# A token mixer on one core: paired w2 products, another scratch layout, later tables and another table of places

## The chip, the cores and the metric
The kernel runs on one core of a Trainium2 chip. The metric is the device time of one execution in microseconds; the time of a kernel is the median of its runs. The engines are TensorE (PE; its weight loads are PEld), VectorE (DVE), ScalarE (ACT), GpSimd (POOL) and SyncE (SP), which here issues every DMA transfer.

## The reference
The input `x` has 32 images of 96 channels and 56x56 points. Layer 0 is a convolution block. Layer 1 is a token mixer with a Fourier transform over the 3136 tokens of an image, and an MLP. The change lies in layer 1 alone.

```python
x = _L0_conv_ref(x, ...)              # 1x1, depthwise 3x3, 1x1, each with batch norm; plus x
t = _to_tokens(x)                     # (32, 3136, 96)
t = t + _L1_attn_ref(_ln_t(t), ...)
t = t + _L1_ffn_ref(_ln_t(t), ...)    # 96 -> 384 -> 96, factors rounded to an 8-bit float
x = _from_tokens(t, x)

def _L1_attn_ref(x, w1, ..., r, i, rb, ib, w2, ...):
    h = jnp.einsum('bnc,hc->bnh', x, w1)               # 192 columns
    h = jax.nn.relu(_bn(h, ...))
    X = jnp.fft.fft(h, axis=1, norm='ortho')
    rd = jnp.diagonal(r)
    idg = jnp.diagonal(i)
    xr = jax.nn.relu(X.real * rd - X.imag * idg + rb)
    xi = jax.nn.relu(X.imag * rd + X.real * idg + ib)
    y = jnp.fft.ifft(xr + 1j * xi, axis=1, norm='ortho').real.astype(jnp.float32)
    o = jnp.einsum('bnh,ch->bnc', y, w2)
    return _bn(o, ...)
```

## The kernel before
The convolution stages come first and leave `z3_scratch`. Then `tokens_stage` takes the images one by one. The Fourier transform of 3136 = 56 x 56 tokens is done in two stages of small products each way; since `h` is real, 29 frequencies `k1` of the first axis are enough. An image passes these steps:

- `load_in`, `act_bn3`, `pool_y`: seven chunks of 8 rows are loaded, batch-normed and added; `store_t` keeps the sum in HBM for the residual.
- `mean1`, `act_square1`, `square1`, `dve_var1`, `act_std1`, `row1`: the statistics of the first layer norm. `row1` (`load_row`, four small transfers) puts the standard deviations into row 96 of `y`.
- `w1` (14 products of 193 columns in pairs), `dve_rstd1`, `act_h`, `stage1`, `act_a`, `store_a`: in seven pieces, w1 with the layer norm, then the first transform stage into `bank_w_s`; ScalarE copies the piece into one of the two halves of `a`, and SyncE stores it to `a_scratch`. The rows of `a` are (q, k): q is one of four groups of 32 rows, k the frequency. A piece may overwrite its half once the piece two before it has landed in HBM (`a_scalar` waits for `st_a[p - 2]`).
- `load_b`: four transfers load `bt` back as (q, j) rows, a run of 192 elements for each row and frequency. The first waits until all seven pieces have landed.
- `spectrum` (6 groups; those named wide take the channels 128 to 191, two frequencies in one product), `act_scaled`, `dve_real`, `pool_imag`, `act_relu`, `dve_fold`: the second transform stage into `bank_x`, the diagonal weights and the ReLU. `fold_vector` writes `zp` (channels 0 to 127, one slot a frequency) or `zq` (wide: channels 128 to 191 of two neighbouring frequencies in the two halves of the rows).
- `w2` (8 groups of four frequencies, the last of one), `dve_wz`, `stage3`, `dve_c`, `store_c`, `load_d`: the w2 product into `bank_c`, a copy to `wz`, the first stage of the way back, a copy to `cc`, and a second trip through HBM, `c_scratch`.
- `stage4` (7 chunks of four products), `dve_residual`: the last stage into `bank_o`; VectorE adds the residual `tb`. There is one `bank_o`, so each chunk of stage 4 waits for the residual before it.
- `mean2` to `dve_rstd2`, `spread_mean`, `spread_rstd`, `dve_centre`, `dve_norm`: the second layer norm; the spread products bring mean and rstd to all channel rows, and VectorE centres (`xc`) and norms (`yq`).
- `mlp1`, `act_h16`, `dve_bias1`, `dve_relu1`, `mlp2`, `act_o`, `dve_bias2`, `pool_out`, `store_out`: the MLP and the output.

Each engine's order is a table of numbers. `PLACES` gives every part of every step a place; a turn is `NT` = 2000 places, a place of 4321 stands for place 321 of the turn two after the image entered. An engine runs through the places of a turn and does what stands there for each of the five images in flight (`LAGS`), as the `..._turn` functions show. Nothing is timed: an engine takes the next step in this order and waits on its semaphores. So a step that waits holds up all that follows on its engine, on SyncE the transfers too.

Before the first turn, SyncE waits for three constants that VectorE sets (`s_init`, among them the memset of `d`), loads six tables (`t1c` 896 KB, `t4c` 1568 KB, `g2c`, `g3c`, and two parts of `sel_d`), and only then the first image. TensorE and VectorE wait for all tables (`s_const`) before their first turn.

The w2 product of a group before; `w2q` holds the weights of the channels 128 to 191 twice, for the upper half of the rows in its columns 0 to 95 and for the lower half in 96 to 191, with zeros elsewhere:

```python
        for j, k1 in enumerate(ks_of(u)):
            o, e = CB[0:TP, 0, j * C:j * C + C], k1 % 2
            nc.tensor.matmul(o, zp[:, k1 // 8 % 2, k1 % 8, :], w2p[:, :], start=True, stop=False)
            ins = nc.tensor.matmul(o, zq[:, k1 // 2 % 8, :], w2q[:, e * C:e * C + C], start=False, stop=True)
```

## Time and profile before

| | before |
|---|---|
| median of 3 runs | 5265.94 us (5251.65 to 5277.84) |
| the profiled execution | 5252.71 us, span 5250.9 us |
| TensorE clock, mean of the span | 0.958 |
| busy share PE / PEld / DVE / ACT / POOL | 91 / 61 / 68 / 65 / 49% |
| DMA: bytes moved, mean rate | 1072 MB, 204 GB/s |
| tokens stage | 2567 us to the end |

The span runs from the first to the last instruction, the time of an execution lies a little above it. A view of windows gives for each stretch how long each engine was busy; the table of waits gives how long an engine stood idle before a line, and whose result ended the wait; the chain of waits is followed back from the last instruction. In a timeline a row stands for a run of like instructions: its start, the time from its start to its end, and in brackets the idle time of the engine before it. A clock of 1.00 is 2.4 GHz and 0.50 is 1.2 GHz.

### The profile page before, as it was taken

Reading aid. Unit: us, or ns where it says so; the run is one execution under the profiler, and the core shown is the slowest. Engines: PE = TensorE matmul, PEld = TensorE weight load, DVE = VectorE, ACT = ScalarE, POOL = GpSimd, SP = SyncE. Lnnn points to the kernel's source line nnn. Section 1 sums busy time; section 2 is a strip of 40 time slices with the busy share of each in tenths; the row PEclk is TensorE's granted clock in tenths of the full one; section 3 lists DMA queues with packets and bytes.
Section 4 is the critical chain, followed back from the end, with each engine's and each line's share of the span. In section 5 each row is a group of like instructions: output and inputs, shape, how many; then the busy total and the mean of one; then the engine's idle time right before and its main releaser. Section 6 shows DMA issues by size and latency. Waiting matters only on the chain.

```text
span 5250.9 us, 153775 instructions
## 1 busy us (share of the span) xinstructions
PE 4775.0 (91%) x63188; PEld 3204.1 (61%) x63188; DVE 3551.9 (68%) x6475; ACT 3387.4 (65%) x5511; POOL 2574.2 (49%) x1508
## 2 busy tenths in 40 slices
PE   8989999999999989999678888888898898889886
PEld 8955555555555544444356666666666666666663
DVE  1156776776778766777427777777777777777776
ACT  4455655565566568888447667676677676777663
POOL 0067777777777756666323333333333333334331
PEclk9989999999999999999769999999999999999997
DMA  7656776777777689999556676776776766776762
GB/s 159 164 144 178 192 182 181 192 183 182 191 185 186 172 315 415 412 419 418 212 146 176 182 183 176 190 182 180 188 187 178 187 182 179 193 184 181 188 156 64
DMA packets 505463, 1072.16 MB, mean 204 GB/s; under 512 B 182240, under 2 KB 330240, under 8 KB 471872
## 3 DMA queue, kind: packets, MB, share of 16 engines
q1 hardware_dynamic: 504768, 1062.33, 70.7%
q8 instruction: 505, 8.27, 0.7%
q14 instruction: 190, 1.56, 0.1%
HBM read 557.40 MB, written 484.44 MB: 198 GB/s over the span
## 4 chain that ended last, share of the span: by engine, by line
PE 31%; DVE 8%; DMA 6%; issue 4%; ACT 2%; SPq 1%; POOL 0%; DVEq 0%; POOLq 0%; ACTq 0%
PE bank_w_s L1456 6%; DMA bt<-a_scratch 4%; PE bank_o L1434 3%; PE bank_w_s L1465 3%; PE bank_x L1409 3%; PE bank_c L1417 3%; PE bank_c L1418 2%; PE bank_c L1424 2%; PE bank_x L1406 2%; PE bank_l L1333 2%; PE bank_l L1390 1%; PE bank_o L1445 1%; DVE zq L1693 1%; PE bank_l L1349 1%; DVE wz L1794 1%
## 5 line engine op out<-in xcount | busy, mean ns | idle before, releaser
L772 POOL TENSOR_TENSOR hlo<-h,hhi 128x1682 f16<-128x1682 f32 x288 | 977.6, 3394 | 376.8 <-DVE hhi L825 376.8
L785 DVE BATCH_NORM_STATS2 stats<-z 128x6 f32<-128x392 f32 x1152 | 597.1, 560 | 437.9 <-ACT z L725 427.8
L735 ACT ACTIVATE h<-c1ps,s 128x1568 f32<-128x1568 f32 x288 | 479.3, 1664 | 629.3 <-PE c1ps L651 629.3
L683 PE MATMUL dwps<-hhi,taps 64*64 64x392 f16 x13824 | 692.9, 331 | 9.5 <-issue 9.4
L683 PE MATMUL dwps<-hlo,taps 64*64 64x392 f16 x13824 | 684.5, 328 | 4.4 <-issue 4.4
L1649 POOL TENSOR_TENSOR s_plus<-d_minus,imag_scaled 128x448 f32<-128x448 f32 (+1 forms) x192 | 203.6, 1060 | 897.1 <-ACT imag_scaled L1516 897.1
L1658 POOL TENSOR_TENSOR onat<-tb,o 96x448 f32<-96x448 f32 x224 | 262.7, 1173 | 643.3 <-DVE o L1718 643.3
L930 ACT ACTIVATE z2m<-z2m,s 128x784 f32<-128x784 f32 x512 | 489.5, 1029 | 104.0 <-DMA z2m<-z_scratch 103.4
L954 POOL TENSOR_TENSOR h_split<-z2m,h_split 128x1568 f16<-128x1568 f32 x128 | 405.2, 3166 | 264.6 <-DVE h_split L993 264.6
L683 PEld LDWEIGHTS dwps<-hhi,taps 64*64 64x64 f16 x13824 | 381.1, 106 | 251.1 <-issue 104.9
L683 PEld LDWEIGHTS dwps<-hlo,taps 64*64 64x64 f16 x13824 | 406.4, 106 | 185.3 <-issue 7.3
L1592 ACT ACTIVATE h<-bank_w_s,rt 128x192 f32<-128x192 f32 x896 | 319.9, 425 | 141.0 <-DVE rt L1724 138.4
L1642 POOL TENSOR_TENSOR y<-zin,x_tok 96x448 f32<-96x448 f32 x224 | 302.2, 1362 | 200.9 <-ACT zin L1598 196.3
L1456 PE MATMUL bank_w_s<-w1a,y 97*128 97x193 f32 x1792 | 381.4, 358 | 15.9 <-ACT a L1586 8.4
L1531 ACT ACTIVATE h<-bank_l 128x448 f16<-128x448 f32 x672 | 340.2, 542 | 80.8 <-PE bank_l L1390 72.6
L201 POOL TENSOR_TENSOR xlo<-xin,x_packed 96x448 f16<-96x448 f32 x224 | 233.7, 1044 | 287.6 <-ACT x_packed L192 287.5
L966 PE MATMUL pps<-z2m,w3T 128*96 128x392 f32 x1024 | 360.4, 495 | 15.1 <-ACT z2m L930 15.1
L1456 PEld LDWEIGHTS bank_w_s<-w1a,y 97*128 97x128 f32 x1792 | 334.0, 211 | 43.2 <-ACT a L1586 14.1
L1417 PE MATMUL bank_c<-w2p,zp 128*112 128x96 f32 x1856 | 347.8, 270 | 10.0 <-DVE cc L1802 10.0
L1418 PE MATMUL bank_c<-w2q,zq 128*112 128x96 f32 x1856 | 337.1, 264 | 0.0
L1434 PE MATMUL bank_o<-t4c,d 128*96 128x112 f32 x1792 | 246.9, 286 | 98.0 <-DVE tb L1748 93.4
L1586 ACT ACTIVATE a<-bank_w_s 128x768 f32<-128x768 f32 x224 | 181.7, 811 | 223.9 <-PE bank_w_s L1465 219.1
(234 smaller groups left out, 10110.9 us busy)
## 6 DMA issues: line engine op xcount, KB each, us to landing
z_scratch<-z SPq DMA_DIRECT2D x1152, 196.0 KB, 3.3
z2m<-z_scratch SPq DMA_DIRECT2D x64, 1960.0 KB, 15.9
...
a_scratch<-a SPq DMA_DIRECT2D x896, 96.0 KB, 1.9
...
t_scratch<-y SPq DMA_DIRECT2D x32, 1344.0 KB, 6.4
c_scratch<-cc SPq DMA_DIRECT2D x128, 336.0 KB, 3.7
d<-c_scratch SPq DMA_DIRECT2D x128, 336.0 KB, 3.9
```

The costliest lines, as they stand in the source:

```text
L683: ins = nc.tensor.matmul(dw[64 * j:64 * j + 64, r, g, 0:QN], taps[half, u, da, dx, :, :].rearrange("p y c -> p (y c)"), part[half, s, a0:a ...
L735: nc.scalar.activation(to, src, ACT.Relu, bias=s1[:, 1, u:u + 1], scale=s1[:, 0, u:u + 1]).then_inc(h_ready, 1)
L772: nc.gpsimd.tensor_tensor(to, h, hi, ALU.subtract).then_inc(lo_ready, 1)
L785: nc.vector.bn_stats(stats[:, i, v, at:at + 6], z2[:, v % 3, g, r, :]).then_inc(s_stat, 1)
L930: nc.scalar.activation(v, v, ACT.Relu, bias=s2[:, 1, t:t + 1], scale=s2[:, 0, t:t + 1]).then_inc(h2_ready, 1)
L954: nc.gpsimd.tensor_tensor(lo, h32, hi, ALU.subtract).then_inc(lo_ready, 1)
L966: nc.tensor.matmul(banks[m], w3T[:, t, :], z2m[:, c // 2, 4 * m + t, cols], start=(t == 0), stop=False)
L1417: nc.tensor.matmul(o, zp[:, k1 // 8 % 2, k1 % 8, :], w2p[:, :], start=True, stop=False)
L1418: ins = nc.tensor.matmul(o, zq[:, k1 // 2 % 8, :], w2q[:, e * C:e * C + C], start=False, stop=True)
L1434: ins = nc.tensor.matmul(OB[0:C, 0, k * TP:k * TP + TP], d[:, j, :], t4c[:, j, :], start=True, stop=True)
L1456: ins = nc.tensor.matmul(WS[:, g % 2, e * (H + 1):(e + 1) * (H + 1)], both, w1a[:, :], start=True, stop=True)
L1531: nc.scalar.activation(h16[:, c % 2, q, :], LL[k % 2][:, 0, 0:CH], ACT.Copy).then_inc(h16_done, 1)
```

## The change
Four things.

**The w2 product** of a group begins with the `zq` part, two frequencies at once: `zq` of a pair is the stationary operand and 192 columns of `w2q` the moving one, so that both frequencies' columns of `bank_c` are written by one product. Then each frequency's `zp` part is added. A group of four has 2 products of 192 columns and 4 of 96 where it had 8 of 96.

**The first scratch** becomes `(NB, 128, NJ, H)`, by the rows of `a` as they lie. A piece is stored by one transfer of 128 rows instead of four of 32, and `load_b` issues four transfers of 28 rows, one for each q, instead of one of 112.

**The tables** come behind the first image: `t1c` after chunk 3, the others after chunk 6, each with its own semaphore, which is waited for where it is first used. SyncE starts at once, and the memset of `d` is the last of the three.

**The places** are all new (of the table two lines are shown).

```diff
-    a_d = nc.dram_tensor("a_scratch", (NB, KP, 4, NJ, H), F32, kind="Internal").ap()
+    a_d = nc.dram_tensor("a_scratch", (NB, 128, NJ, H), F32, kind="Internal").ap()
...
-PLACES = {'load_in': (790, 792, 1059, 1276, 1342, 1628, 1944),
...
+PLACES = {'load_in': (212, 561, 689, 855, 903, 940, 974),
...
-    s_const, s_init, s_sel, s_settled = sem("tables_loaded"), sem("constants_set"), sem("rows_table"), sem("settled")
+    s_init, s_sel, s_settled = sem("constants_set"), sem("rows_table_loaded"), sem("settled")
+    s_t1, s_g, s_t4 = sem("t1_loaded"), sem("g2_g3_loaded"), sem("t4_loaded")
...
         sp.dma_start(xin[:, c % 3, :], x[n, :, cols]).then_inc(ld_in[c % 3], 16)
+        if isinstance(n, int) and n == 0:
+            load_tables(sp, c)
+
+    def load_tables(sp, c):
+        if c == 3:
+            sp.dma_start(t1c[:, :, :], t1_d.rearrange("p (j c) -> p j c", j=NJ)).then_inc(s_t1, 16)
+        if c == 6:
+            sp.dma_start(g2c[:, :], g2_d).then_inc(s_g, 16)
+            sp.dma_start(g3c[:, :], g3_d).then_inc(s_g, 16)
+            sp.dma_start(t4c[:, :, :], t4_d.rearrange("p (j c) -> p j c", j=NJ)).then_inc(s_t4, 16)
...
         if k == 0:
             for p in range(NP4):
-                sp.wait_ge(st_a[p], f * 64 + 64)
+                sp.wait_ge(st_a[p], f * 16 + 16)
...
-        src = a_d[f, k0:k0 + n].rearrange("k q j c -> (q j) k c")
-        sp.dma_start(bt[:, k0:k0 + n, :], src).then_inc(ld_b[k], 16)
+        for q in range(4):
+            src = a_d[f, 32 * q + k0:32 * q + k0 + n].rearrange("k j c -> j k c")
+            sp.dma_start(bt[NJ * q:NJ * q + NJ, k0:k0 + n, :], src).then_inc(ld_b[k], 16)
...
-        for q in range(4):
-            v = a[32 * q:32 * q + 32, (par + p) % 2, :, :].rearrange("k b x -> k (b x)")
-            to = a_d[f, :, q, 4 * p:4 * p + 4, :].rearrange("k j c -> k (j c)")
-            sp.dma_start(to, v).then_inc(st_a[p], 16)
+        v = a[:, (par + p) % 2, :, :].rearrange("p b x -> p (b x)")
+        sp.dma_start(a_d[f, :, 4 * p:4 * p + 4, :].rearrange("p j c -> p (j c)"), v).then_inc(st_a[p], 16)
...
     def _(sp):
-        sp.wait_ge(s_init, 3)
         sp.dma_start(im_t[:, :, :, :].rearrange("p a s c -> p (a s c)")[:, 0:4 * C], sel_d[:, 0:4 * C]).then_inc(s_sel, 16)
-        sp.dma_start(t1c[:, :, :], t1_d.rearrange("p (j c) -> p j c", j=NJ)).then_inc(s_const, 16)
-        sp.dma_start(t4c[:, :, :], t4_d.rearrange("p (j c) -> p j c", j=NJ)).then_inc(s_const, 16)
-        sp.dma_start(g2c[:, :], g2_d).then_inc(s_const, 16)
-        sp.dma_start(g3c[:, :], g3_d).then_inc(s_const, 16)
-        sp.dma_start(part[:, :], sel_d[:, 4 * C:4 * C + 2]).then_inc(s_const, 16)
+        sp.dma_start(part[:, :], sel_d[:, 4 * C:4 * C + 2]).then_inc(s_sel, 16)
         turns(sp, sync_turn)
...
-        for j, k1 in enumerate(ks_of(u)):
-            o, e = CB[0:TP, 0, j * C:j * C + C], k1 % 2
-            nc.tensor.matmul(o, zp[:, k1 // 8 % 2, k1 % 8, :], w2p[:, :], start=True, stop=False)
-            ins = nc.tensor.matmul(o, zq[:, k1 // 2 % 8, :], w2q[:, e * C:e * C + C], start=False, stop=True)
+        ks = ks_of(u)
+        for j in range(0, len(ks), 2):
+            w = len(ks[j:j + 2]) * C
+            nc.tensor.matmul(CB[0:TP, 0, j * C:j * C + w], zq[:, ks[j] // 2 % 8, :], w2q[:, 0:w], start=(j == 0),
+                             stop=False)
+        for j, k1 in enumerate(ks):
+            ins = nc.tensor.matmul(CB[0:TP, 0, j * C:j * C + C], zp[:, k1 // 8 % 2, k1 % 8, :], w2p[:, :],
+                                   start=False, stop=(j == len(ks) - 1))
...
     def _(dve):
-        nc.vector.memset(d[:, :, :], 0.0).then_inc(s_init, 1)
         nc.vector.memset(y[:, :, :, :, W:64], 1.0).then_inc(s_init, 1)
         nc.vector.memset(va[:, :, :], 1.0).then_inc(s_init, 1)
-        dve.wait_ge(s_sel, 16)
+        nc.vector.memset(d[:, :, :], 0.0).then_inc(s_init, 1)
+        dve.wait_ge(s_sel, 32)
```

What the new places do to the order is seen at three places of a steady turn. The first is VectorE at the start of stage 4: `tb` is the residual, `zq` the wide fold, `va` the variance of the next image, `rt` the reciprocal for its w1. Before:

```order
L1699 TENSOR_SCALAR va<-va 128x4x56
L1718 TENSOR_SCALAR o<-o,fqb 96x448
L1748 SCALAR_TENSOR_TENSOR tb<-bank_o,w2shift,tb 96x8x56
L1693 SCALAR_TENSOR_TENSOR zq<-d_minus,s_plus 128x8x56 x2
L1748 SCALAR_TENSOR_TENSOR tb<-bank_o,w2shift,tb 96x8x56 x2
L1724 RECIPROCAL rt<-bank_w_s 128x2
```

and after:

```order
L1718 TENSOR_SCALAR va<-va 128x4x56
L1737 TENSOR_SCALAR o<-o,fqb 96x448
L1767 SCALAR_TENSOR_TENSOR tb<-bank_o,w2shift,tb 96x8x56 x3
L1712 SCALAR_TENSOR_TENSOR zq<-d_minus,s_plus 128x8x56 x2
L1743 RECIPROCAL rt<-bank_w_s 128x2
```

The wide fold moved from behind the first residual to behind the third. TensorE's order around it is the same in both: three chunks of stage 4, four w1 products, a chunk, w2 group 0.

The second is where the MLP of one image begins beside the w2 groups 2 and 3 of the next. On TensorE, from the spread of the rstd (`rstd_parts`) to the first mlp1 (`yq`), before:

```order
L1362 MATMUL bank_l<-rstd_parts,sel 96x224 x4
L1465 MATMUL bank_w_s<-h,t1c 64x192 x8
L1390 MATMUL bank_l<-yq,fq 128x448 x2
L1456 MATMUL bank_w_s<-w1a,y 128x193 x4
L1390 MATMUL bank_l<-yq,fq 128x448
L1424 MATMUL bank_c<-wz,g3c 112x384
```

and after:

```order
L1371 MATMUL bank_l<-rstd_parts,sel 96x224 x4
L1485 MATMUL bank_w_s<-h,t1c 64x192 x8
L1440 MATMUL bank_c<-wz,g3c 112x384
L1400 MATMUL bank_l<-yq,fq 128x448 x2
L1474 MATMUL bank_w_s<-w1a,y 128x193 x2
```

Stage 3 of group 2 moved ahead of the first mlp1. A little later on VectorE, from the last wide fold (`zq`, 7 slots) to the copy `wz` of w2 group 3 and the second pair of centrings (`xc`), before:

```order
L1693 SCALAR_TENSOR_TENSOR zq<-d_minus,s_plus 128x7x56 x2
L1724 RECIPROCAL rt<-bank_w_s 128x2
L1794 COPY wz<-bank_c 112x384
L1724 RECIPROCAL rt<-bank_w_s 128x2
L1729 TENSOR_TENSOR xc<-tb,bank_l 96x448 x2
```

and after:

```order
L1813 COPY wz<-bank_c 112x384
L1724 TENSOR_SCALAR h<-h,fqb 128x448
L1743 RECIPROCAL rt<-bank_w_s 128x2
L1748 TENSOR_TENSOR xc<-tb,bank_l 96x448 x2
L1743 RECIPROCAL rt<-bank_w_s 128x2
L1821 COPY cc<-bank_c 112x384
L1757 TENSOR_TENSOR yq<-xc,bank_l 96x448 x2
L1731 TENSOR_SCALAR hq<-h 128x1344
L1712 SCALAR_TENSOR_TENSOR zq<-d_minus,s_plus 128x7x56 x2
```

The fold moved behind the copy, the centrings and the norms.

The third is SyncE, from the sixth store of `a` to the first two loads of `bt`, before:

```order
L1275 DMA a_scratch<-a 32x768 x4
L1268 DMA tb<-t_scratch 96x512
L1254 DMA c_scratch<-cc 112x8x96
L1268 DMA tb<-t_scratch 96x512
L1275 DMA a_scratch<-a 32x768 x4
L1261 DMA d<-c_scratch 32x2688
L1249 DMA bt<-a_scratch 112x8x192
L1254 DMA c_scratch<-cc 112x8x96
L1249 DMA bt<-a_scratch 112x8x192
```

and after:

```order
L1268 DMA c_scratch<-cc 112x8x96
L1287 DMA a_scratch<-a 128x768
L1275 DMA d<-c_scratch 32x2688
L1287 DMA a_scratch<-a 128x768
L1282 DMA tb<-t_scratch 96x512
L1263 DMA bt<-a_scratch 28x8x192 x4
L1282 DMA tb<-t_scratch 96x512 x2
L1263 DMA bt<-a_scratch 28x8x192 x4
```

The load of `d` moved ahead of the last store of `a`, and the store of `cc` between the two loads of `bt` is gone from there. Also on SyncE, the store of the image (`t_scratch<-y`, 1344 KB) moved from between the fifth and the sixth store of `a` to between the second and the third:

```order
L1287 DMA a_scratch<-a 128x768
L1268 DMA c_scratch<-cc 112x8x96
L1293 DMA t_scratch<-y 96x3584
L1287 DMA a_scratch<-a 128x768
```

These last rows are of after; in a turn all seven chunks of the next image are loaded ahead of them, where before the last chunk was loaded three stores later.

## Rows read from the trace of the kernel before

**Rows 1.** The page, busy time and share of the span of TensorE, with its instructions.
```profile
PE 4775.0 (91%) x63188; PEld 3204.1 (61%) x63188; DVE 3551.9 (68%) x6475; ACT 3387.4 (65%) x5511; POOL 2574.2 (49%) x1508
```
**Rows 2.** Row transfers on SyncE (first and last start), and ten steady turns by engine.
```profile
L1239 SPq DMA_DIRECT2D y<-va x128: 511/657/731, 2603.3 to 5044.7; - x128
...
3947.00:4737.00 790.00, 708.13 (x6597) 531.72 (x6596) 588.63 (x1225) 556.59 (x1036) 300.50 (x260) 0.97 0.70 184
```
**Rows 3.** Waits of TensorE in these ten turns: us in total, times, longest.
```profile
PE bank_o L1434 <- DVE tb L1748: 28.5, 20, 2.1
...
PE bank_x L1409 <- DMA bt<-a_scratch: 5.5, 8, 1.2
```
**Rows 4.** The chain of waits, w2 and w1 products: start, us, instructions merged.
```profile
4228.73 0.20 PE bank_c L1417 x2
...
4263.05 2.27 PE bank_w_s L1456 x8
...
4271.06 1.32 PE bank_w_s L1456 x8
```
**Rows 5.** Timeline of VectorE, residuals and folds of a steady turn.
```profile
4258.47 2.20 DVE L1693 SCALAR_TENSOR_TENSOR zq<-d_minus,s_plus 128x448 f32<-128x448 f32 x2
4260.59 0.67 DVE L1748 SCALAR_TENSOR_TENSOR tb<-bank_o,w2shift,tb 96x448 f32<-96x448 f32 x1
...
4298.61 1.76 DVE L1693 SCALAR_TENSOR_TENSOR zq<-d_minus,s_plus 128x392 f32<-128x392 f32 x2 [1.22 <-PE bank_c L1418]
```
**Rows 6.** Timeline of TensorE in the same turn, with its waits in brackets.
```profile
4258.53 1.01 PE L1434 MATMUL bank_o<-t4c,d 128*96 128x112 f32 x8 [0.84 <-DVE tb L1748]
4261.32 1.73 PE L1434 MATMUL bank_o<-t4c,d 128*96 128x112 f32 x8 [1.78 <-DVE tb L1748]
...
4291.74 0.54 PE L1390 MATMUL bank_l<-yq,fq 96*128 96x448 fp8e5 x2 [0.72 <-DVE yq L1738]
...
4300.96 0.90 PE L1424 MATMUL bank_c<-wz,g3c 112*112 112x384 f32 x2 [0.67 <-DVE wz L1794]
4302.17 0.44 PE L1362 MATMUL bank_l<-rstd_parts,sel 12*96 12x224 bf16 x4 [0.32 <-DVE xc L1729]
```
**Rows 7.** Timeline of the start and of a steady turn, issues on SyncE.
```profile
2603.26 2.75 SPq L1239 DMA_DIRECT2D y<-va  x4
2607.11 2.94 PE L1456 MATMUL bank_w_s<-w1a,y 97*128 97x193 f32 x8 [5.89 <-DMA y<-va]
...
4257.03 2.59 SPq L1239 DMA_DIRECT2D y<-va  x4
...
4311.94 2.12 SPq L1275 DMA_DIRECT2D a_scratch<-a  x4
```
**Rows 8.** The chain's transfers; the page's: count, KB each, median us to landing.
```profile
4233.86 1.89 DMA a_scratch<-a
...
4235.99 6.00 DMA bt<-a_scratch
...
a_scratch<-a SPq DMA_DIRECT2D x896, 96.0 KB, 1.9
...
t_scratch<-y SPq DMA_DIRECT2D x32, 1344.0 KB, 6.4
...
x_tok<-in_x_dram SPq DMA_DIRECT2D x224, 168.0 KB, 3.9
```
**Rows 9.** Timeline of the start of the tokens stage.
```profile
2566.81 2.30 DVE L1840 MEMSET d<- 128x2688 f32 x1 [1.13 <-PEq L870]
...
2570.35 0.33 SPq L1310 DMA_DIRECT2D imag_scaled<-table_sel  x1
...
2581.49 0.76 ACT L1598 ACTIVATE zin<-zin,s 96x448 f32<-96x448 f32 x1 [16.82 <-DMA x_tok<-in_x_dram]
```
**Rows 10.** Timeline of ScalarE, copies of pieces 3 and 5 into `a`.
```profile
4284.89 0.81 ACT L1586 ACTIVATE a<-bank_w_s 128x768 f32<-128x768 f32 x1 [1.78 <-PE bank_w_s L1465]
...
4296.79 0.81 ACT L1586 ACTIVATE a<-bank_w_s 128x768 f32<-128x768 f32 x1
```

135 lines of the change are left out of this document (72 added, 63 removed).

## The prediction
> **What bounds the kernel now.** I read the page first: TensorE is busy 91% of the span [rows 1]. The change lies in the tokens stage, which begins at 2567 us with the first memset [rows 9] and runs 32 images through a pipeline, one per turn. The LN1 row transfer of the first image is issued at 2603.3 and the last at 5044.7 [rows 2]; less the 2 us between the first and the fourth transfer of a row, that is 2439 us in 31 turns, 78.7 us a turn. In ten steady turns (790 us) TensorE is busy 708 us, VectorE 589, ScalarE 557, and the DMA engines 70% [rows 2]. So TensorE is the bound and waits 8.2 us a turn. The table of TensorE's waits says on whom [rows 3]: 28.5 us in ten turns on the residual of VectorE (stage 4 and the residual hand one bank back and forth) and 5.5 on the loads of `bt`; smaller ones stand singly in [rows 6]. An edit pays if it shortens TensorE's work or one of these waits, and only so far as nothing else is late by then.
>
> **The w2 product.** Before, each of the 29 frequencies takes two products of 96 columns, each with its own weights; the trace has two instructions for one fp32 product. In the chain such a pair takes 0.20 us, 98 ns an instruction, while eight instructions of 193 columns take 1.32 us, 165 ns each [rows 4]. 165 ns for 193 columns would be 82 ns for 96, so at 96 columns something other than the columns sets the pace; the weights in between are what is left. A group of four frequencies has 16 instructions: 16 x 98 = 1.57 us. After, it has 4 of 192 columns and 8 of 96: 4 x 165 + 8 x 98 = 1.44 us. That is 0.13 us less in each of seven full groups, **0.9 us a turn**. Bounds: 0, if a column costs 98/96 ns in these products whatever the weights; 1.8 us, if the eight narrow ones ran at 82 ns (1.57 - 0.66 - 0.66 = 0.25 us a group). I stay at 0.9, because the narrow ones keep their own weights.
> The Trainium skill (TensorE: Matmul & The Clock Gate, The mechanism) says that weight loads overlap running matmuls only where the row groups differ, and (LDWEIGHTS) gives P/1.2 ns for P columns, an estimate of 93 ns for our 112. Strictly in series with an 82 ns product that would be 175 ns an instruction; the trace has 98 [rows 4], so here they overlap and the measurement decides. In series, the 14 saved loads (28 instructions) would be worth 2.6 us a turn instead of 0.9.
>
> **Stage 4 and the wide fold.** At this place VectorE does one residual, then the two `zq` halves of the fold (2.20 us), then the next residual [rows 5]; TensorE's third stage 4 waits 1.78 us for that residual [rows 6]. After, the fold stands behind three residuals. The second stage 4 starts at 4258.53, takes 0.95, the residual 0.6 and the handover 0.1: the third starts at 4260.2 instead of 4261.32, **1.1 us earlier**. The next work, w1 of the new image, needs the row transfer: in turn 0 TensorE starts 1.1 us after the last of the four issues has ended (2606.01, 2607.11), and here that gives 4257.03 + 2.59 + 1.1 = 4260.7 [rows 7], before TensorE comes (4261.1). What is late next is the folded `zq`: the third residual ends at about 4261.8, the fold at 4264.0, and w2 comes behind four w1 products (1.3) and a stage 4 (0.8), at 4263.3: a new wait of 0.7, which I reduce to 0.5, because part of the w1 work there runs at the lower clock. VectorE's reciprocals for w1 stand behind the fold too and delay ScalarE's `h`, whose user, stage 1, comes only after w2 and another stage 4. Price: 1.1 - 0.5 = **-0.6**, bounds -1.8 and 0.
>
> **The waits before mlp1 and behind w2 group 3.** TensorE waits 0.72 us for `yq` before the first mlp1 [rows 6]. After, stage 3 of group 2 stands in this gap (an 0.8 us piece whose `wz` was copied before the norms), **-0.7**. Further on VectorE waits 1.22 us with the last wide fold for w2 group 3 and folds for 1.76 us, and only then copies `wz` [rows 5]; stage 3 waits 0.67 and the spread of the rstd 0.32 [rows 6]. After, the copy and the two centrings come first and the fold later; w2 group 4, its user, is still over 4 us away. **-1.0**. Bounds of both together: 0 and -1.7.
> Sum so far: 0.9 + 0.6 + 0.7 + 1.0 = 3.2 us a turn.
>
> **The first scratch.** Four stores of 96 KB become one of 384 KB, and each load of 672 KB becomes four of 168 KB. The last piece's path is the one that matters: TensorE's last stage 1, the copy, store, wait, load, spectrum. Four issues take 2.12 us of SyncE [rows 7], and the last store lands 1.89 us after its issue [rows 8]; one issue takes 0.3, and between 1.9 us for 96 KB and 6.4 for 1344 KB [rows 8] the line gives 2.9 for 384 KB. So 4.0 becomes 3.2 us: -0.8. The load: 6.00 us where it is clear [rows 8]; four issues put its last quarter 1.0 to 1.3 us behind the first, but the bytes and runs are the same and the first starts as before; I take +0.5, bounds 0 and +1.3. The load of `d` that stood between the last store and the load (the order above) is issued before it now, which takes 336 KB out of the way: up to -0.5. Together about -0.8, but the path also has less work to hide behind: two w2 groups (0.3) lie on it. SyncE's order elsewhere: in the new one the 1344 KB store of the image stands ahead of the third store of `a`, the fourth load of `bt` behind the sixth image chunk; both have slack (below). I book 0 for the whole path and +0.3 for the shortened cover, bounds -0.55 (today's wait for `bt` at the first spectrum group is gone [rows 3]) and +1.5.
> The Trainium skill (DMA: Bandwidth & Descriptors, Why a DMA increments its semaphore by 16 and not by 1) says a transfer uses the largest number of engines up to 16 that divides its outermost size: 16 for the old 112, 14 for the new 28. No row here shows such a size. By this rule the 6.00 us become 6.9.
>
> **The start.** SyncE no longer waits for the memsets, and the tables do not stand ahead of the image: the first transfer goes at 2566.8 instead of 2570.35, four issues less are ahead, and the first chunk, used at 2581.49 [rows 9], comes some 10 us sooner. But the 896 KB table lies between chunks 3 and 4, and the 1568 KB table plus the image's store ahead of the row transfer. I take **-6 us once**, bounds -10 and 0.
>
> **The sum.** 3.2 a turn, less 0.3 for the `bt` cover, less 0.4 because three of the w2 groups lie in a stretch where VectorE is the late one (the chain between two loads of `bt` runs over it), makes 2.5; 31 turns give 78 us, and with the start 84. The profiled execution took 5252.7 us (span 5250.9), so 5169. It stands 13 us under the median of the three runs (5265.9), at their low end; of this I add half, 6: **5175 us**.
>
> **Rivals.**
> *The clock gives back more.* In the steady turns the granted clock is 0.97 on average [rows 2]: 6% of the time at 1.2 GHz, 4.7 us a turn, 2.4 of them lost. One such stretch begins at 4261, right behind the two waits of stage 4: eight w1 instructions take 2.27 instead of 1.32 us [rows 4]. The change removes waits right ahead of it and of the next (4302, behind the waits of 0.67 and 0.32). If both stretches go, 31 x 2.4 = 74 us: 5101; half of it, 5138. For it: the places agree. Against: some waits remain at both (0.8 and 0.7 us in stage 4). Chance 0.12.
> *Gains absorbed.* Store of `a` number 3 now stands behind the 1344 KB store. ScalarE's copy of piece 5 into the same half waits for its landing; today the copies of pieces 3 and 5 start at 4284.89 and 4296.79, 11.9 us apart [rows 10]; 0.8 for the copy, 6.4 and 2.9 for the transfers make 10.1. For it: DMA is busy 70%. Chance 0.18.
> *The new places do nothing, the w2 product gains 0.* The waits wander to the next late engine, as VectorE is busy 75%: start and little else, 5240 to 5275. Against: the four places are read one by one. Chance 0.13.
> *Slower: the quarter loads run one behind the other.* If each of the four costs what a 168 KB transfer costs alone, 3.9 us [rows 8], a load of `bt` takes 15.6 instead of 6.0: +9.6 on a path that TensorE already waits for, less 2.5: +7.1 a turn, 5175 + 31 x 9.6 = 5473. It decides from a load longer by 3.5 us on, where the 84 us are eaten and 26 more lost. Against: four stores are issued within 2.12 us and the last lands 1.89 us after its own issue [rows 7, 8], so transfers of one queue overlap. Chance 0.07.
> *The forecast*, 5135 to 5215: 0.50.
>
> **How the numbers follow.** The range 5095 to 5240 holds the forecast, the clock and the absorbed case: 8 in 10. A measurement of this kernel can tell 0.5% from no change, 26 us: below 5239.6 is faster, 0.80; up to 5292 the same, 0.13; above, slower, 0.07.
>
> **What would show it.** Rows of a steady turn: w2 groups of 12 instructions in 1.44 us and 165 ns for the wide ones; stage 4's wait on the residual at 1.8 us a turn instead of 2.85, and at most 0.7 of a new wait of w2 for `zq`; no wait of stage 3 behind w2 group 3 nor of the first mlp1; waits for `bt` below 1.5 us a turn; a turn of 76.2 us; the first w1 at about 2601 instead of 2607. I am wrong if the waits are gone and the turn is still over 77 (then look at ScalarE's copy of piece 5 and at the loads of `bt`), or if the wide products take over 190 ns.

## The result and the profile after

| | before | after |
|---|---|---|
| median | 5264.56 us (5251.65 to 5277.84, 4 runs) | 5099.26 us (5094.76 to 5113.47, 4 runs) |
| span of the profiled execution | 5250.9 us | 5092.8 us |
| TensorE clock, mean of the span | 0.958 | 0.972 |

The ratio is 0.9697, with an interval of 0.9679 to 0.9714: 3.0% faster. The forecast was 5175 us with a range of 5095 to 5240. The direction was right and the time lies inside the range, at its edge; but the gain is 165 us where its sum had 84 (5175 stands 90 under the median before).

The page after, TensorE and the other engines [as rows 1], and the row transfers on SyncE [as rows 2]:
```profile
PE 4692.9 (92%) x62292; PEld 3120.1 (61%) x62292; DVE 3398.0 (67%) x6475; ACT 3389.3 (67%) x5511; POOL 2513.4 (49%) x1508
...
L1252 SPq DMA_DIRECT2D y<-va x128: 510/658/732, 2596.5 to 4887.3; - x128
```
A turn takes (4887.3 - 2596.5 - 2) / 31 = 73.8 us instead of 78.7: 4.9 less, where 2.5 was forecast. The first row transfer goes at 2596.5 instead of 2603.3: 6.8 once, where 6 was forecast. 31 x 4.86 + 6.8 is 157.5 of the 158.1 us between the spans, so nearly all of it is in the turn.

To see where a turn changed I took 25 turns, the fifth to the twenty-ninth, of every kernel, with the mean length of a turn as the measure. The view of windows gives them in one row each: stretch, its length, busy time of TensorE, its weight loads, VectorE, ScalarE, GpSimd, then clock, DMA share, GB/s. Before, then after:
```profile
2918.10:4885.30 1967.20, 1764.62 (x16370) 1323.36 (x16369) 1461.44 (x3043) 1378.57 (x2568) 746.79 (x647) 0.96 0.70 184
```
```profile
2891.80:4737.60 1845.80, 1702.67 (x15679) 1257.56 (x15678) 1339.45 (x3047) 1383.64 (x2575) 699.58 (x649) 0.99 0.74 196
```
Divided by 25: TensorE was busy 70.6 us and idle 8.1; now it is busy 68.1 and idle 5.7. So the gain has two halves, 2.5 less work and 2.4 less waiting. The table of TensorE's waits in ten turns (us in total, times, longest), 3830 to 4568 in after [as rows 3]:
```profile
PE bank_o L1452 <- DVE tb L1767: 17.6, 20, 1.7
PE bank_x L1421 <- DMA bt<-a_scratch: 8.8, 10, 1.7
PE bank_l L1342 <- ACT sq L1573: 8.1, 10, 0.8
PE bank_c L1440 <- DVE wz L1813: 7.9, 19, 0.7
PE bank_l L1400 <- ACT h L1550: 4.8, 9, 0.5
PE bank_l L1371 <- DVE xc L1748: 4.8, 10, 0.5
```
And four lines of the same table of before, 3947 to 4737, that [rows 3] does not show:
```profile
PE bank_c L1424 <- DVE wz L1794: 14.2, 25, 0.9
PE bank_l L1390 <- DVE yq L1738: 6.7, 10, 0.7
PE bank_l L1362 <- DVE xc L1729: 3.1, 10, 0.3
PE bank_x L1406 <- DMA bt<-a_scratch: 2.8, 5, 1.0
```
The residual `tb` cost 28.5 and costs 17.6, as foreseen (2.85 to 1.8 a turn). The waits for `yq` are gone. Those for the copy `wz` fell from 14.2 to 7.9. `bt`, two lines in before, costs as much as it did: 8.3 and 8.8.

The clock has a part of its own. The trace's record of the granted clock, added up over the same 25 turns as their own row transfers cut them (in before from 2908.4 to 4883.3 us), has 146.8 us at 1.2 GHz before, in 32 stretches, and 30.7 us in 7 after: 5.9 and 1.2 us a turn. A stretch at half clock costs at most half its length, so at most 2.9 and 0.6 us a turn are lost.

### The profile page after: what moved, and what is told of

Its sections match the earlier page's. It is cut to its first block, busy times and chain, and to the rows that moved or that the text cites. A ratio compares the mean times of both kernels' runs of the same rounds, so it can differ in the third digit from the quotient of the medians.

```text
span 5092.8 us, 151731 instructions
## 1 busy us (share of the span) xinstructions
PE 4692.9 (92%) x62292; PEld 3120.1 (61%) x62292; DVE 3398.0 (67%) x6475; ACT 3389.3 (67%) x5511; POOL 2513.4 (49%) x1508
## 3 DMA queue, kind: packets, MB, share of 16 engines
q1 hardware_dynamic: 499136, 1062.31, 72.5%
## 4 chain that ended last, share of the span: by engine, by line
PE 32%; DMA 8%; DVE 5%; issue 2%; ACT 1%; SPq 1%; POOL 1%; DVEq 0%; POOLq 0%; ACTq 0%
PE bank_w_s L1474 6%; PE bank_o L1452 4%; PE bank_x L1421 4%; DMA bt<-a_scratch 3%; PE bank_w_s L1485 3%; PE bank_c L1440 2%; PE bank_c L1433 2%; PE bank_c L1430 2%; DMA a_scratch<-a 2%; PE bank_l L1400 2%; PE bank_l L1342 2%; DMA tb<-t_scratch 1%; PE bank_x L1418 1%; PE bank_l L1358 1%; PE bank_l L1371 1%
## 5 line engine op out<-in xcount | busy, mean ns | idle before, releaser
L1677 POOL TENSOR_TENSOR onat<-tb,o 96x448 f32<-96x448 f32 x224 | 236.4, 1062 | 620.8 <-DVE o L1737 620.8
L1661 POOL TENSOR_TENSOR y<-zin,x_tok 96x448 f32<-96x448 f32 x224 | 254.5, 1149 | 313.8 <-ACT zin L1617 313.6
L1550 ACT ACTIVATE h<-bank_l 128x448 f16<-128x448 f32 x672 | 342.8, 543 | 77.4 <-PE bank_l L1400 65.4
L1474 PEld LDWEIGHTS bank_w_s<-w1a,y 97*128 97x128 f32 x1792 | 308.5, 197 | 53.6 <-issue 20.2
L1767 DVE SCALAR_TENSOR_TENSOR tb<-bank_o,w2shift,tb 96x448 f32<-96x448 f32 x224 | 152.3, 680 | 251.4 <-PE bank_o L1452 211.7
L825 DVE CAST hhi<-h 128x1682 f16<-128x1682 f32 x288 | 297.7, 1034 | 9.0 <-ACT h L740 9.0
L1452 PE MATMUL bank_o<-t4c,d 128*96 128x112 f32 x1792 | 224.9, 270 | 64.7 <-DVE tb L1767 57.2
L1421 PE MATMUL bank_x<-g2c,bt 112*128 112x112 f32 x1856 | 244.1, 285 | 41.8 <-DMA bt<-a_scratch 35.5
```

Source lines behind the costliest of these rows:

```text
L1421: ins = nc.tensor.matmul(xs[:, s, 0:TP], bt[:, k0 + s, 0:128], g2c[:, :], start=True, stop=True)
L1452: ins = nc.tensor.matmul(OB[0:C, 0, k * TP:k * TP + TP], d[:, j, :], t4c[:, j, :], start=True, stop=True)
L1474: ins = nc.tensor.matmul(WS[:, g % 2, e * (H + 1):(e + 1) * (H + 1)], both, w1a[:, :], start=True, stop=True)
L1550: nc.scalar.activation(h16[:, c % 2, q, :], LL[k % 2][:, 0, 0:CH], ACT.Copy).then_inc(h16_done, 1)
```

## The experiments, one part at a time

Every kernel below was timed beside the kernel before, on one chip in each group. The budget of a turn is from the same kind of row as above: "busy" and "idle" are TensorE's, "low" the time at 1.2 GHz in the clock's record, in us a turn. It comes from one profiled execution of each kernel. Most of these lie within 12 us of the median; that of scratch_only lies 20 us above it, that of new_aps 18 above, that of filled_best 17 below. 20 us are 0.6 us a turn.

| kernel | median, us | ratio to before (interval) | turn | busy | idle | low |
|---|---|---|---|---|---|---|
| before | 5258.6, 5251.7, 5249.9 | | 78.7 | 70.6 | 8.1 | 5.9 |
| after (above) | 5099.3 | 0.9697 (0.9679 to 0.9714) | 73.8 | 68.1 | 5.7 | 1.2 |
| w2_only | 5234.7 | 0.9966 (0.9950 to 0.9982) | 78.3 | 69.6 | 8.6 | 6.1 |
| after_old_w2 | 5120.6 | 0.9743 (0.9722 to 0.9763) | 74.3 | 68.8 | 5.5 | 1.0 |
| places_only | 5096.0 | 0.9697 (0.9675 to 0.9719) | 73.6 | 68.7 | 5.0 | 0.3 |
| scratch_only | 5275.9 | 1.0035 (1.0019 to 1.0051) | 79.9 | 71.1 | 8.7 | 7.1 |
| after_old_scratch | 5085.5 | 0.9678 (0.9651 to 0.9706) | 73.5 | 68.0 | 5.4 | 1.4 |
| new_pe_dve | 5526.2 | 1.0517 (1.0486 to 1.0548) | 87.2 | 73.0 | 14.1 | 13.1 |
| new_aps | 5376.0 | 1.0234 (1.0203 to 1.0265) | 82.7 | 72.5 | 10.2 | 11.3 |
| filler | 5205.7 | 0.9903 (0.9876 to 0.9930) | 77.4 | 70.8 | 6.5 | 2.6 |
| three_moves | 5190.2 | 0.9881 (0.9858 to 0.9903) | 76.4 | 69.0 | 7.4 | 1.0 |
| light_y | 5191.3 | 0.9877 (0.9853 to 0.9901) | 76.5 | 69.0 | 7.5 | 0.0 |
| pool_busy | 5110.6 | 0.9728 (0.9705 to 0.9750) | 74.3 | 68.1 | 6.2 | 0.8 |
| filled_best | 5077.2 | 0.9654 (0.9630 to 0.9678) | 73.1 | 68.7 | 4.3 | 0.3 |

The three medians of before belong to the three groups of kernels; light_y stood beside 5254.0.

**Each part alone.** First the four parts. `w2_only` is before with the new body of `w2_tensor` (the hunk with `ks_of` in the diff), `after_old_w2` takes it back out of after.

> The kernel before with the new w2 product alone. Theory A (each edit is worth its own term): a group costs 1.42 us instead of 1.57, 0.9 to 1.0 us a turn, so 28 to 30 us less: a ratio near 0.9945. The w2 groups lie at other moments than in the changed kernel, but none waits more. Theory B (part of the gain comes from the clock): shorter products alone remove no wait, so the low-clock time of the steady turns stays at about 147 us, and no more than the 30 us is gained. Rival (not path): part of the w2 groups lie where VectorE is late, the gain is under 15 us. Against both theories: a gain above 50 us.

> The changed kernel with the w2 product of before. Theory A: 0.9 to 1.0 us a turn dearer, 28 to 30 us above the changed kernel, 5127 to 5130, as w2_only is below before. Theory B (the last part of the gain is over-proportional, since waits and slow clock come back): 40 us or more above. Rival (in the new order the w2 groups lie under waits for other engines): under 15 us above.

A group in the timeline of TensorE in after, 4 wide instructions, 8 narrow, and the next work:
```profile
4152.76 0.82 PE L1430 MATMUL bank_c<-w2q,zq 128*112 128x192 f32 x4
4153.41 0.94 PE L1433 MATMUL bank_c<-w2p,zp 128*112 128x96 f32 x8
4154.18 0.93 PE L1452 MATMUL bank_o<-t4c,d 128*96 128x112 f32 x8
```
From 4152.76 to 4154.18 is 1.42 us; 1.44 was forecast. The busy time of a turn falls by 0.95 in w2_only, the booked 0.9. But idle time rises by 0.5, and the turn gives only 0.4. In time that is 18 us by the ratio (24 by the medians) in w2_only, and 24 by the two ratios (21 by the medians) with and without it in the new table: below the 28 to 30 that were expected, above the 15 of the "not path" rival. The "not path" rival had a part of it: what TensorE no longer works, it partly waits.

`places_only` has only after's table of places.

> The kernel before with the new places alone: scratch, w2 product and tables as before. Theory A: 165 us less the 30 of w2 and the 7 of the start, near 128 us if the scratch is worth nothing: a ratio near 0.976. Theory B: of this 128, 50 to 55 us appear as less time at 1.2 GHz (147 us of low-clock records before, 38 in the changed kernel), and VectorE's wide folds take about 610 ns instead of 1078, since another engine's work stands beside them. If the low-clock time falls to about 40 us here, the places did it; if it stays near 147, it came from the w2 product or the scratch. Rival (the new order needs the new scratch, because four stores and their issues stand badly in it): under 80 us gained, with waits on the stores of a or on bt that the changed kernel doesn't have.

This one kernel has the whole gain: ratio 0.9697 like after, 163 us. Its 25 turns, and its waits for `bt` between 2900 and 4740 us:
```profile
2885.80:4726.80 1841.00, 1716.53 (x16399) 1274.38 (x16400) 1336.62 (x3049) 1382.43 (x2573) 699.85 (x650) 1.00 0.75 197
...
PE bank_x L1409 <- DMA bt<-a_scratch: 3.3, 8, 0.7
```
The low-clock time falls to 0.3 us a turn, so the places did that, as theory B of the expectation said; the gain itself is above the 128 us that both theories had. VectorE's busy time falls too, from 58.5 to 53.5 us a turn, with the same instructions.

`scratch_only` has only the new layout of the first scratch (the hunks on `a_d`, `load_b` and `store_a`); `after_old_scratch` takes it out of after.

> The kernel before with the new layout of the first scratch alone, one store a piece, four loads of 28 rows a group. As predicted: store 2.9 to 3.9 us instead of 1.9 but one issue instead of four, the load some tenths later, in sum 0 for the path: within 15 us of before. The changed kernel showed a store of 3.9 us, so the last piece's path would be 0.3 + 3.9 = 4.2 instead of 4.0: slower by 0 to 1 us a turn, 0 to 31 us. Rival (the quarter loads are uneven, 6.0 becomes 6.9): +0.9 us a turn more wait for bt, 28 us slower. Rival (the scratch is a gain, since SyncE has fewer issues for stores): 20 us or more faster.

> The changed kernel with the scratch of before: four stores of 32 rows a piece, one load of 112 rows a group. The new scratch alone made the kernel 18 us slower (ratio 1.0035). If that adds up here: 5078 to 5085, a ratio near 0.966 to before, and the wait for bt falls from 8.8 us in ten turns to 1 or 2, as with the new places alone. Rival (the new order was made for one store a piece, and the 4 issues now hold up SyncE): 5095 to 5120. This one is the candidate to beat both kernels.

The layout costs 17 us alone (ratio 1.0035). In the new table it costs 14 by the medians and 10 by the ratios, whose intervals overlap. Chain of waits of after, last store and last quarter of the load, then of after_old_scratch, last of four stores and whole load:
```profile
4118.83 3.05 DMA a_scratch<-a
4123.40 5.18 DMA bt<-a_scratch
```
```profile
4114.07 1.88 DMA a_scratch<-a
4116.19 4.81 DMA bt<-a_scratch
```
And SyncE's issues in the same places, after first:
```profile
4118.83 0.34 SPq L1287 DMA_DIRECT2D a_scratch<-a  x1
...
4122.12 1.69 SPq L1263 DMA_DIRECT2D bt<-a_scratch  x4
```
```profile
4112.66 1.84 SPq L1288 DMA_DIRECT2D a_scratch<-a  x4
...
4116.19 0.32 SPq L1262 DMA_DIRECT2D bt<-a_scratch  x1
```
From the first issue of the store to the first of the load 3.29 us with the new layout, 3.53 with the old: only 0.24 saved, because the 384 KB store takes 3.05 in this turn. The page of after has an even longer median for all pieces:
```profile
a_scratch<-a SPq DMA_DIRECT2D x224, 384.0 KB, 3.9
```
From there to the landing of the load's last byte 4123.40 + 5.18 - 4122.12 = 6.46 against 4.81: 1.65 lost, 1.28 of it the three issues ahead of the last quarter. In this turn the path is 1.4 us longer. The saved issues of the store come back as issues of the load, at the place where all wait for it. The waits for `bt` between 2900 and 4740 us (23 to 25 turns), of before, scratch_only, after_old_scratch, after and, in one of its two lines, w2_only:
```profile
PE bank_x L1409 <- DMA bt<-a_scratch: 12.3, 16, 1.8
PE bank_x L1406 <- DMA bt<-a_scratch: 6.0, 10, 1.0
```
```profile
PE bank_x L1405 <- DMA bt<-a_scratch: 27.4, 23, 2.3
PE bank_x L1408 <- DMA bt<-a_scratch: 7.0, 15, 1.1
```
```profile
PE bank_x L1422 <- DMA bt<-a_scratch: 15.7, 21, 2.1
```
```profile
PE bank_x L1421 <- DMA bt<-a_scratch: 19.4, 25, 1.7
PE bank_x L1418 <- DMA bt<-a_scratch: 3.5, 8, 0.7
```
```profile
PE bank_x L1406 <- DMA bt<-a_scratch: 17.1, 19, 1.9
```
Alone the layout adds 16 us of waiting in these 23 turns, and 1.2 us of low clock a turn come on top, in an execution 20 us above the median: both are upper ends. In the new table it adds 7. These rows also show where a part of the w2 gain goes. w2_only differs from before in the product alone and waits 21.6 us for `bt` (the line above and one of 4.5) instead of 18.3, and 39.3 for `wz` instead of 32.2. In the new table after waits 22.9 for `bt` and after_old_w2 17.1; with the new places alone it is 3.3, and after_old_scratch, which has the w2 product and the later tables besides, waits 15.7. TensorE gets sooner to a load and a copy that do not come sooner. after_old_scratch came out at the upper end of what was expected (5078 to 5085), but its wait for `bt` did not fall to 1 or 2 us in ten turns; it is 6.3.

**Halves of the table.** Is the gain in TensorE's and VectorE's order, which the prediction read? `new_pe_dve` has their new places alone, `new_aps` those of ScalarE, GpSimd and SyncE:
```diff
-PLACES = {... all of before ...}
+PLACES = {... the steps of the named engines from after, the others from before ...}
```

> The kernel before with the new places of TensorE and VectorE alone; ScalarE, GpSimd and SyncE in their old order. The new places as a whole took 163 us off. Theory A (the waits that the prediction read are VectorE's and TensorE's, so their two orders carry the gain): at least two thirds, 105 to 160 us less, the low-clock time gone, while the wide fold of 128x448 stays near 1078 ns where GpSimd's order decides it and falls to about 613 where VectorE's does. Theory B (the other engines' orders carry it: when the image chunks, the sums of GpSimd and the copies of ScalarE come): under 60 us less, new waits of TensorE on ScalarE or on VectorE.

> The other half: the new places of ScalarE, GpSimd and SyncE, with TensorE and VectorE in their old order. Theory A: within 25 us of before, since the waits for the residual (28 us in ten turns), for wz and for yq stay. Theory B: 100 us or more less. If the halves add up to 163 us they are independent; if each alone gives little or costs time, the new table works only as a whole.

Theories A and B fell in both: each half makes the kernel slower, by 5.2% and 2.3%. Only the last clause of the second expectation, that the new table works only as a whole, is what came. Waits of TensorE in 3830 to 4568 (eight to nine of their longer turns), of new_pe_dve and of new_aps:
```profile
PE bank_x L1353 <- DMA bt<-a_scratch: 41.4, 8, 6.0
PE bank_l L1334 <- ACT h L1475: 27.5, 27, 1.8
```
```profile
PE bank_c L1368 <- DVE wz L1738: 42.0, 18, 4.0
```
In new_pe_dve TensorE arrives at loads and copies that the old ScalarE and SyncE deliver for the old order; in new_aps it waits 42.0 us on VectorE's `wz`. This table of places works only as a whole, so its gain can't be assigned to an engine by swapping its column. One thing can be. The wide fold of 128x448 takes 1055 ns in the mean in new_pe_dve, where VectorE's order is new, and 660 in new_aps, where GpSimd's is: its length follows the other half.

**The moves that were priced.** `three_moves` is before with the three moves of the prediction and nothing else:
```diff
- 'dve_fold': (4921, 5169, 5369, 6006, 6128, 6490)
+ 'dve_fold': (4921, 5231, 5369, 6006, 6183, 6490)
- 'dve_wz': (5402, 5647, 5970, 6133, ...)     'stage3': (5603, 5656, 5908, ...)
+ 'dve_wz': (5402, 5647, 5970, 6127, ...)     'stage3': (5603, 5656, 5790, ...)
```

> The kernel before with only the moves that the prediction priced: the wide fold of group 1 behind the third residual, stage 3 of group 2 ahead of the first mlp1, the copy wz of group 3 and the centrings ahead of the fold of group 4. All else as before. Theory A (the sum by terms): 0.6 + 0.7 + 1.0 = 2.3 us a turn, less 0.4 for the late VectorE, 59 us off: a ratio near 0.989. Theory B (much of the new table's worth lies in steps that the prediction did not read): under 40 us, with the fold of group 1 still at 1.08 us an instruction (GpSimd works beside it at the new place too), w2 group 0 waiting about 1 us for zq, and the low-clock time little changed. Rival (the clock multiplies it): over 90 us.

5190 us, 60 to 62 less (ratio 0.9881), and 76.4 us a turn, 2.25 less than before: the time is what theory A had, 59 us. Its turn is not: theory A had 2.3 less 0.4, so 1.9 a turn. 31 turns of 2.25 would be 70 us, and 9 of them are lost again behind the last row transfer (217 us to the end instead of 208). And the budget says that the agreement is an accident. Idle time fell by 0.7 a turn, not by 1.9; busy time fell by 1.6, with the same instructions, and the low-clock time from 5.9 to 1.0 us. Its window row, its wait for the residual, and waits in 3830 to 4568 (9.7 turns) that are new or longer:
```profile
2907.60:4818.60 1911.00, 1725.55 (x16383) 1281.04 (x16382) 1456.26 (x3049) 1374.72 (x2571) 747.72 (x647) 0.99 0.72 190
...
PE bank_o L1378 <- DVE tb L1692: 16.8, 18, 1.3
PE bank_x L1353 <- DVE d_minus L1626: 5.6, 10, 1.6
PE bank_l L1306 <- DVE xc L1673: 5.0, 10, 0.5
PE bank_c L1361 <- DVE zq L1637: 4.9, 5, 1.1
```
The wait for the residual fell as foreseen, and new waits on VectorE took most of it: for `zq`, for `d_minus`, for `xc`. The rest of the turn's gain, 1.6 us of busy time, came through the clock.

**The clock by itself.** `filler` adds work to before where TensorE stands still, and moves nothing:
```diff
+            for _ in range({1: 3, 2: 8}.get(c, 0)):
+                nc.tensor.matmul(CB[0:C, 0, 0:64], w2p[0:C, 0:C], w2q[0:C, 0:64], start=True, stop=True)
             pe.wait_ge(t2_done, b * NCH + c)
```

> The kernel before with 3 and 8 added fp32 products of 96x64 into a bank that is idle then, ahead of the waits for the residual in the second and the third chunk of stage 4 (0.84 and 1.78 us): TensorE works there instead of standing still, and nothing else changes; their output is not used. The added 11 products are 22 instructions, at 90 to 98 ns 2.0 to 2.2 us a turn for 2.6 us of waits. Theory B (the clock falls where TensorE has stood still, and this is worth 50 us): the stretches at 1.2 GHz behind stage 4 go, the mean granted clock of the steady turns rises from 0.97 to 0.98 or more, and the kernel is 15 to 60 us faster although it does more. Theory A (the clock is a bystander): same or up to 20 us slower, clock unchanged.

The kernel does 352 more products and is 46 us faster (ratio 0.9903, 51 us by it). A steady turn of it on TensorE:
```profile
4227.96 0.65 PE L1432 MATMUL bank_c<-w2q,w2p 96*96 96x64 f32 x6
4229.29 1.01 PE L1436 MATMUL bank_o<-t4c,d 128*96 128x112 f32 x8 [0.69 <-DVE tb L1750]
4230.13 1.50 PE L1432 MATMUL bank_c<-w2q,w2p 96*96 96x64 f32 x16
4232.27 1.01 PE L1436 MATMUL bank_o<-t4c,d 128*96 128x112 f32 x8 [0.64 <-DVE tb L1750]
4233.11 1.49 PE L1458 MATMUL bank_w_s<-w1a,y 97*128 97x193 f32 x8
```
The w1 products behind stage 4 take 1.49 us here. In the turn of before that the prediction quotes the timeline has them longer, and its stage 4 too:
```profile
4262.85 2.47 PE L1456 MATMUL bank_w_s<-w1a,y 97*128 97x193 f32 x8
```
The time at 1.2 GHz falls from 5.9 to 2.6 us a turn, half of that is 1.6, and the turn is 1.3 shorter. The budget closes: the added work is some 2.0 us a turn (22 instructions at 90 ns, an estimate), idle time fell by 1.6, and busy time rose by 0.2 only, so some 1.8 us came back through the clock. So theory B holds: standing still ahead of and in stage 4 brings 3.3 of the 5.9 us of low clock, and these cost time on the path. What brings the other 2.6 this run does not show. The same fillers (3 and 3) on the best kernel:

> The changed kernel with the scratch of before, and 3 + 3 added products of 96x64 into the idle bank ahead of the second and the third chunk of stage 4, where 0.88 and 0.77 us are waited for the residual. Without them it took 5085.5 us. Theory B (the clock): its mean of the steady turns is 0.99, the stretches that are left at 1.2 GHz cost some 19 us; if the fillers remove them, 5065 to 5075. Rival: there is nothing left to win and 6 x 0.2 = 1.2 us a turn for 1.65 us of waits don't fit beside the handovers: 5085 to 5100.

5077 us, ratio 0.9654 (0.9630 to 0.9678), against 0.9678 (0.9651 to 0.9706) without them in another group: the intervals overlap, so this gain of 8 to 13 us is likely but not settled, and it stays just short of the 5065 to 5075 of theory B. Its turn is 73.1 instead of 73.5, its low-clock time 0.3 instead of 1.4; that turn is from the fastest of its five executions. Both are below after; filled_best is the fastest kernel of the study, 0.4% under after.

**VectorE beside GpSimd.** In after the wide folds are much shorter. Groups of VectorE by shape over the whole span (mean ns behind the busy time), before, then after:
```profile
L1705 DVE TENSOR_SCALAR h<-h,fqb 128x448 f16<-128x448 f16 x672 | 281.4, 442 | 9.1 <-ACT h L1531 8.1
L1693 DVE SCALAR_TENSOR_TENSOR zq<-d_minus,s_plus 128x448 f32<-128x448 f32 x64 | 65.1, 1056 | 7.9 <-ACT s_plus L1524 7.6
```
```profile
L1724 DVE TENSOR_SCALAR h<-h,fqb 128x448 f16<-128x448 f16 x672 | 224.1, 356 | 37.9 <-ACT h L1550 37.4
L1712 DVE SCALAR_TENSOR_TENSOR zq<-d_minus,s_plus 128x448 f32<-128x448 f32 x64 | 36.7, 613 | 0.0
```
The trace says what stood beside them. In before 62 of the 64 instructions of this fold run beside an operation of GpSimd and take 1070 ns in the mean, the other two 613; in after none of the 64 does. The operation on `h` takes 326 ns in both kernels where no GpSimd operation stands beside it, and 645 and 432 in the mean where one does.

`pool_busy` is after with three more sums on GpSimd ahead of the second `pool_y` of a turn, beside the fold:
```diff
+        if c == 1:
+            for k in range(3):
+                nc.gpsimd.tensor_tensor(extra[:, k + 1, :], extra[:, 0, :], extra[:, 0, :], ALU.add)
         pool.wait_ge(bn3_done, n * NCH + c + 1)
...
+        nc.gpsimd.memset(extra[:, 0, :], 1.0).then_inc(s_extra, 1)
+        pool.wait_ge(s_extra, 1)
```

> The changed kernel with three added GpSimd sums of 96x448 in each turn, between the first and the second sum of an image chunk, where GpSimd stands idle for 5.3 us and the wide fold of group 1 runs in 1.15 us; their output is not used and nobody waits for them. Theory A (VectorE's operations with two inputs in SBUF wait for GpSimd's, one at a time): the fold's two instructions take 1.0 to 1.1 us each instead of 0.61, the fold ends 1 us later, w2 group 0 waits up to 0.7 us for zq: 10 to 30 us slower in all. Rival (the two engines don't disturb one another, the 1078 ns came from something else, such as the DMA load): fold unchanged at 0.61, time within 5 us. The Trainium skill (SBUF: State Buffer, on the shared port pair) says that GpSimd and a VectorE operation with two SBUF inputs lock one another out for a whole instruction; that is the side of theory A.

VectorE, GpSimd and TensorE at that place:
```profile
4154.38 2.24 DVE L1719 SCALAR_TENSOR_TENSOR zq<-d_minus,s_plus 128x448 f32<-128x448 f32 x2
```
```profile
4153.05 3.09 POOL L1659 TENSOR_TENSOR extra<-extra 96x448 f32<-96x448 f32 x3
```
```profile
4156.68 0.91 PE L1432 MATMUL bank_c<-w2q,zq 128*112 128x192 f32 x4 [0.85 <-DVE zq L1719]
```
The two fold instructions take 2.24 us where after has 1.15, and w2 waits 0.85 for them; the turn is 0.5 longer, the kernel 0.3% slower than after by the ratios, whose intervals just overlap. Theory A holds. GpSimd's three sums are 0.93, 0.93 and 1.31 us long; 0.93 is the length of 69 of the 96 added sums, so the third is stretched too: the two engines take turns, and each waits for the other. The Trainium skill (SBUF — State Buffer, SBUF: two separate sides) says that GpSimd and a VectorE operation with two SBUF inputs exclude one another for whole instructions; the 2.24 us agree.

Is this also the rest, the 2.8 us a turn between three_moves and places_only? `light_y` takes most of GpSimd's image sum away from three_moves. It leaves out seven of the eight rows of each chunk; VectorE fills `y` with ones at the start instead:
```diff
-        nc.gpsimd.tensor_tensor(to, v, xv, ALU.add).then_inc(y_done, 1)
+        nc.gpsimd.tensor_tensor(to[:, 0:1, :, :], v[:, 0:1, :, :], xv[:, 0:1, :, :], ALU.add).then_inc(y_done, 1)
...
-        nc.vector.memset(y[:, :, :, :, W:64], 1.0).then_inc(s_init, 1)
+        nc.vector.memset(y[:, :, :, :, :], 1.0).then_inc(s_init, 1)
```

> The kernel with the three moves, in which GpSimd's sum of an image chunk is cut to one of its eight rows (56 of 448 elements a channel); the rest of the image is left out, and VectorE fills y with ones once at the start, some 8 us more. Five sixths of this GpSimd work goes, 7 x 1.36 us a turn become some 7 x 0.2, while TensorE, VectorE and ScalarE have the same instructions in the same order. The three moves took a turn from 78.7 to 76.4 us, all new places to 73.6; TensorE's idle time went to 7.4 and 5.0. Theory A (the rest of the new table's gain is VectorE, which GpSimd no longer stretches: 58.2 to 53.5 us a turn): VectorE's busy time falls to 54 to 56 a turn, the wide fold of 448 to 613 ns, and the turn to 74 to 75. Rival (VectorE's longer operations have cover, the rest lies in the order of the steps): VectorE's busy time falls as well, the turn stays at 76.0 or more.

```profile
2908.10:4821.35 1913.25, 1724.57 (x16416) 1275.89 (x16414) 1439.65 (x3053) 1378.57 (x2577) 573.25 (x652) 1.00 0.72 190
```
In this window row GpSimd's work falls from 29.9 to 22.9 us a turn, VectorE's only from 58.3 to 57.6, and the turn stays at 76.5. Neither side can claim it: VectorE's time did not fall as both had it. At the fold's new place it is not the image sum that stands beside it but the sums of the spectrum, as GpSimd's timeline in three_moves shows, with VectorE's fold 3975.45 to 3977.81:
```profile
3974.73 1.13 POOL L1593 TENSOR_TENSOR s_plus<-d_minus,imag_scaled 128x448 f32<-128x448 f32 x1
3975.82 1.51 POOL L1594 TENSOR_TENSOR d_minus<-d_minus,imag_scaled 128x448 f32<-128x448 f32 x1
```
So the image sum is ruled out as the cause, and whether VectorE's shorter operations carry the other 2.8 us stays open. What the tables of waits do say is where they lie: from three_moves to places_only the waits for `zq`, `d_minus`, `yq`, `wz` and `cc`, all VectorE's, fall by 2.1 us a turn together, and those for `bt` by 0.5. One thing light_y shows in passing: it has no low-clock time at all in its 25 turns, three_moves has 1.0 us a turn, and both turns are equal. So this last part of the low clock was not worth its half here; what the filler won with its 3.3 us a turn can't be scaled down to it. In three_moves, too, busy time fell by 1.6 us for 4.9 less at 1.2 GHz, a third and not a half.

## Why the prediction was right and wrong

That 5099 lies in the range is owed to the bound that the clock rival set, not to the forecast's own sum, which has half of the gain.

**The w2 product: right in size, wrong in worth.** 1.44 us a group was forecast and 1.42 measured; 0.9 us a turn booked, 0.95 found in the busy time. The step that failed is taking TensorE's work as the path's: 0.4 us a turn arrived in w2_only, 0.7 to 0.8 in the new table (21 to 24 us). The text knew that `bt` was near (0.3 for the cover, 0.4 for VectorE); these two deductions were right in kind and stand for this term.

**Stage 4 and the fold.** The third stage 4 waits 0.77 us instead of 1.78: booked 1.1, measured 1.0. The new wait of w2 for `zq`, booked at 0.5, does not exist in after, because the fold runs beside an idle GpSimd, in 1.15 us instead of 2.20. In three_moves, where it runs beside GpSimd's sums, it takes 2.36 us, and w2 waits 0.96 in the turn quoted. The price of the fold was read from a row whose length was the neighbour's doing; the order of GpSimd, which the prediction did not look at, decides it.

**The waits for `yq` and behind w2 group 3.** In after both went away at the places that the text names: `yq` is in no line of the table, and stage 3 of group 3 does not wait. But [rows 3]'s table has 14.2 us on `wz` in 25 waits, the second largest, which the text counted under the smaller ones and read in one place; it fell by 0.63 a turn, and the wait of the spread products for `xc` grew by 0.17 where the text had it gone. So this term of 1.0 gave 0.5. In three_moves `yq` keeps 0.5 a turn and other waits grew: 2.3 us a turn booked for the three moves, 0.7 less idle time measured. "What is late next" was asked for the fold alone, not for the other two.

**The clock: the term that was left out, and the step that failed most.** The text had it as a rival at 0.12, all or half of 74 us, and booked 0 in the forecast itself. Measured are 5.9 us a turn at 1.2 GHz before and 1.2 after, at most 2.3 us of lost time. Busy time fell by 2.5 us a turn and the w2 product explains 0.9 of it, so 1.6 us a turn, 50 us, came through the clock (places_only, without the w2 product, has 1.9 less busy time); the filler showed by itself that such time is on the path. The argument against, that 0.8 and 0.7 us of waiting remain in stage 4, was no argument: they do remain in after, and the w1 products behind them run at full clock. With 1.6 a turn booked, the forecast would have been 5125.

The whole miss is then 4.86 - 2.5 = 2.36 us a turn: 1.6 for the clock, and 0.8 for idle time (2.4 less, where 2.3 - 0.7 = 1.6 was booked). The two tables of waits in ten turns say where the 0.8 lies. The new wait for `zq` (booked +0.5), the late VectorE (+0.4) and the shortened cover of `bt` (+0.3, measured +0.05) did not come, the term behind w2 group 3 gave 0.5 less than booked, and waits that the text did not price gave some 0.3 (`cc` and ScalarE's `h` 0.5 less, `hq` 0.2 more). So the text took too much off for what might be late, and too much for one move. Against places_only, which has 3.1 us less idle time than before, w2, scratch and tables together give 0.7 back.

**The first scratch: booked 0, costs 10 to 17 us.** The intervals of the two ratios in the new table overlap, so there the cost is likely, not settled. The store was to take 2.9 us and takes 3.05 in the turn above (median of the page 3.9), and the load was booked at +0.5 with a bound of +1.3; it is 1.65 longer there. The uneven quarters of the absorbed case can't be told from the issues.

**The start.** 6.8 against 6: right. No run has the later tables alone. From VectorE's first memset of the stage to the first row transfer it is 36.5 us in before, 34.6 in places_only and 29.7 in after, so 1.8 us come with the places and the rest with the tables.

**The rivals.** Gains absorbed: no, ScalarE's copies into `a` wait for a store once in the whole stage, 1.2 us. Places do nothing: no, they have the whole gain alone. Quarter loads one behind the other: no, the last quarter lands 5.2 us after its own issue. Clock gives back more: yes, and 5099 is even below its own lower end of 5101, because waits fell more as well.
